# Two more quarters of the array for the values of an attention step, and a new order of the step, on one core

## The reference

```python
qkv = x @ Wqkv; q, k, v = split(qkv)            # 128 -> 3 * 1024
q, k = l2norm(q) * qs, l2norm(k) * ksc          # per head, then rotary with a scale
sim = einsum('bhwie,bhwje->bhwij', bq, bk2) * 8 # a window of 32 looks at itself and the one before
attn = softmax(where(mask, -max, sim))
x = x + einsum('bhwij,bhwje->bhwie', attn, bv2).reshape(b, n, 1024) @ Wo
xn = (x - mu) / sqrt(var + 1e-5) * g + bln
a, gate = split(xn @ W1 + b1)                   # 128 -> 2 * 341
x = x + (a * gelu(gate)) @ W2 + b2
```

## Time and profile before

| | before |
|---|---|
| median of three runs | 2670.35 us (2667.77 to 2670.66) |
| the profiled execution | 2670.37 us, span 2668.6 us |
| TensorE busy | 2405.0 us, 90% |
| ScalarE busy | 1779.9 us, 67% |
| VectorE busy | 1754.0 us, 66% |
| GpSimd busy | 1407.7 us, 53% |
| mean granted clock of TensorE | 0.951 of full speed |

### The profile page before, as it was taken

How to read it: one execution, slowest core, us unless ns; L and a number is a source line. 1 busy time by engine, 2 the same in 40 slices (tenths; PEclk the granted TensorE clock), 3 DMA queues, 4 the chain that set the end, 5 groups by cost and what they waited for, 6 DMA issues and landing times.

```text
span 2668.6 us, 94059 instructions
## 1 busy us (share of the span) xinstructions
PE 2405.0 (90%) x36344; PEld 1671.1 (63%) x36344; DVE 1754.0 (66%) x4841; ACT 1779.9 (67%) x6116; POOL 1407.7 (53%) x1358
## 2 busy tenths in 40 slices
PE   6997899999999999999999999999998676799996
PEld 4664676666666666666666666666666354566662
DVE  3554776777767766777767777777774324788863
ACT  3774677777767776777767777777776142678771
POOL 1664665666556565656565655666563000666650
PEclk9999999999999999999999999999999676899997
DMA  3000112111121113111121113111121100000000
GB/s 96 1 0 3 32 42 76 39 39 39 40 69 41 38 37 77 39 38 38 36 75 38 40 36 79 39 40 38 39 59 36 29 0 4 9 15 16 13 10 20
DMA packets 143994, 97.15 MB, mean 36 GB/s; under 512 B 67112, under 2 KB 138320, under 8 KB 142800
## 3 DMA queue, kind: packets, MB, share of 16 engines
q1 hardware_dynamic: 143568, 91.31, 13.4%
HBM read 23.11 MB, written 1.05 MB: 9 GB/s over the span
## 4 chain that ended last, share of the span: by engine, by line
PE 76%; ACT 9%; issue 7%; DVE 3%; SPq 2%; POOL 1%; DMA 1%; ACTq 0%; POOLq 0%; DVEq 0%
PE bank L668 20%; PE bank L745 10%; PE bank L778 7%; PE bank L689 7%; PE bank L723 5%; PE bank L832 3%; PE bank L823 3%; PE bank L732 3%; PE bank L814 2%; PE bank L390 2%; PE bank L653 2%; PE bank L717 2%; ACT L1252 1%; ACT arena L1252 1%; PE bank L764 1%
## 5 line engine op out<-in xcount | busy, mean ns | idle before, releaser
L1430 POOL TENSOR_TENSOR arena<-arena 128x512 f32<-128x512 f32 x448 | 561.2, 1272 | 416.3 <-DVE arena L1570 416.3
L668 PE MATMUL bank<-wqkv,hs 128*128 128x512 f32 x1344 | 671.1, 609 | 41.1 <-ACT arena L1233 29.0
L1437 POOL TENSOR_TENSOR arena<-arena,rnorm 128x512 f32<-128x512 f32 x448 | 458.8, 1044 | 93.4 <-DVE rnorm L1619 91.3
L1565 DVE TENSOR_TENSOR arena<-bank,rot 128x512 f32<-128x512 f32 x448 | 308.5, 689 | 233.0 <-PE bank L668 216.6
L1204 ACT ACTIVATE arena<-bank,amx 128x64 f32<-128x64 f32 x1536 | 458.4, 336 | 0.3
L1444 POOL TENSOR_TENSOR arena<-arena,ainv 128x512 f32<-128x512 f32 x192 | 200.4, 1044 | 365.5 <-DVE ainv L1642 365.5
L668 PEld LDWEIGHTS bank<-wqkv,hs 128*128 128x128 f32 x1344 | 231.8, 195 | 210.1 <-issue 153.0
L745 PE MATMUL bank<-arena 64*64 64x32 f32 (+1 forms) x9216 | 315.0, 221 | 47.1 <-issue 30.1
L745 PEld LDWEIGHTS bank<-arena 64*64 64x64 f32 x9216 | 291.1, 136 | 101.8 <-issue 60.2
L1204 ACT ACTIVATION_READ_ACCUMULATOR arena<-bank,amx 128x1 f32 x1536 | 353.1, 230 | 0.0
L1233 ACT ACTIVATE arena<-bank 128x512 f32<-128x512 f32 x224 | 133.4, 596 | 321.1 <-PE bank L745 284.4
(11 more groups left out here) (160 smaller groups left out, 3514.8 us busy)
## 6 DMA issues: line engine op xcount, KB each, us to landing
arena<-arena SPq DMA_DIRECT2D x384, 64.0 KB, 2.4
arena<-arena SPq DMA_DIRECT2D x768, 32.0 KB, 1.9
wqkv<-in_L_ffn_Wqkv_dram SPq DMA_DIRECT2D x6, 1024.0 KB, 5.2
hs<-z SPq DMA_DIRECT2D x128, 32.0 KB, 1.8
fx<-z SPq DMA_DIRECT2D x32, 128.0 KB, 2.3
hs<-z SPq DMA_DIRECT2D x128, 31.8 KB, 1.9
fx<-z SPq DMA_DIRECT2D x32, 127.0 KB, 2.5
wqkv<-in_L_ffn_Wqkv_dram SPq DMA_DIRECT2D x24, 128.0 KB, 5.4
```

The lines of the kernel that those rows point to most:

```text
L668: nc.tensor.matmul(bank[o][:], src[:], wqkv[w][:, off:off + 512], start=True, stop=True).then_inc(AT[name] if part < 2 else AT[name][i], 1)
L1430: nc.gpsimd.tensor_tensor(t, t, rs[i][c], ALU.add).then_inc(AT["ak" if c else "aq"][i], 1)
L1437: nc.gpsimd.tensor_tensor(t, t, rnorm[p % 2][:, i, HU * c:HU * c + HU].unsqueeze(2).to_broadcast([P, HU, DH]), ALU.mult).then_inc(AT["mk" ...
L1565: nc.vector.tensor_tensor(heads(rc[i][c][p % 2]), src, r[:, 2 * c, :].unsqueeze(1).to_broadcast([P, HU, DH]), ALU.mult)
```

## The change

Four parts, all in phase 0 alone:
- values_all computes the four chunks in two halves. Chunks 0 and 1 go, as all did, from rows of group g to the columns and partitions of the same numbers in bank 7. Chunks 2 and 3 go to the other partitions (group 0 to 64 to 127, group 1 to 0 to 63) of bank 6. The calls alternate between the four quarters of the array. The number of matmuls is the same.
- In o_t chunks 2 and 3 thus have their partitions swapped. The rows of the output weights are loaded to match, by six DMAs for a layer where there was one. The waits on ld_wo count six.
- outputs copies 256 columns of bank 7 and 256 of bank 6.
- The lists step_0 of TensorE, ScalarE, GpSimd and VectorE have a new order. values_all(0) takes batch s-2 where it took s-3, and so do values_all(1), probs_all(1), project_out, outputs and the residual; scores(0), values(0), exponents(0) and divide(0) take s-1 where they took s-2; turn(1) of queries takes s-1 where it took s-2. Waits follow: the new bank 6 work waits for the copy of the keys and is waited for by the next keys and probabilities. SyncE's list is not changed.

The diff; of the lists the new text alone is shown (the lines taken out are those of the lists printed above):

```diff
@@ -496,8 +496,11 @@
                     sp.dma_start(qks[:, j, :], A[pre + n][i].rearrange("(o d) -> o d", o=1).to_broadcast([P, DH])
                                  ).then_inc(ld_rot, 16)
                 if ph["net"] == 0:
-                    sp.dma_start(wo[w][:].rearrange("p a b n -> p (a b) n"), A[pre + ph["Wo"]][i].rearrange("(j p) n -> p j n", p=P)
-                                 ).then_inc(ld_wo, 16)
+                    wo_ = A[pre + ph["Wo"]][i].rearrange("(u v j p) n -> v p u j n", u=2, v=2, p=P)
+                    for u in range(2):
+                        sp.dma_start(wo[w][:, u, 0:2, :], wo_[0][:, u]).then_inc(ld_wo, 16)
+                        for a in range(2):
+                            sp.dma_start(wo[w][DH * a:DH * a + DH, u, 2:4, :], wo_[1][DH * (1 - a):DH * (1 - a) + DH, u]).then_inc(ld_wo, 16)
                 else:
                     wo_ = A[pre + ph["Wo"]][i].rearrange("(j a g d) n -> a g d j n", a=2, g=2, d=DH)
                     for a in range(2):
...
@@ -738,12 +741,13 @@
                     pe.wait_ge(vd[i], 96 * (p + 1))
                     v, b, c = v_s[i], vb[i][:, 0:256], vb[i][:, 256:512]
                     sources = [((0, 64), (v[:, 0:256], b)), ((64, 96), (c, c)), ((96, 128), (b, v[:, 256:512]))]
-                    for j in range(4):
+                    for j in range(2):
                         for (q0, q1), src in sources:
-                            for g in range(2):
-                                rows = slice(DH * g, DH * g + DH)
-                                mm = nc.tensor.matmul(bank4[7][rows, j, q0:q1], src[g][rows, DH * j:DH * j + DH],
-                                                      pbt[i][0][rows, j * P + q0:j * P + q1], start=True, stop=True)
+                            for half in range(2):
+                                for g in range(2):
+                                    rows, to, h = slice(DH * g, DH * g + DH), DH * (g ^ half), j + 2 * half
+                                    mm = nc.tensor.matmul(bank4[7 - half][to:to + DH, j, q0:q1], src[g][rows, DH * h:DH * h + DH],
+                                                          pbt[i][0][rows, h * P + q0:h * P + q1], start=True, stop=True)
                     mm.then_inc(AT["o"][i], 1)
 
                 def probs(i, p, g):
...
@@ -870,78 +874,83 @@
                         ff_up(f, slot_ - 2, s)
 
                 def step_0(s):
                     if live(s):
                         if live(s - 1):
                             at(pe, AT["sqk"], un(1, s - 1))
                         keys(0, s)
                     if live(s - 2):
                         if live(s - 3):
                             at(pe, AT["res"][0], s - 2)
                         else:
                             at(pe, AT["ve"][0], s - 1)
                         project_in(1, s - 2, 2, 7, "v")
+                        at(pe, AT["qte"][1], s - 1)
+                        probs_all(0, s - 2)
+                    if live(s):
+                        if live(s - 1):
+                            at(pe, AT["sqq"], un(1, s - 1))
+                        queries(0, s)
+                    if live(s - 2):
+                        at(pe, AG["ex"][0][0], s - 1)
+                        at(pe, AG["ex"][0][1], s - 1)
+                        scores_all(1, s - 2)
+                        at(pe, AT["ve"][1], s - 1)
+                        at(pe, AT["kte"][1], s - 1)
+                        values_all(0, s - 2)
+                    feed_forward_0(s, 0)
+                    if live(s):
+                        at(pe, AT["sqk"], un(0, s))
+                        keys(1, s)
+                    if live(s - 1):
                         if live(s - 2):
                             at(pe, AG["pte"][0][0], s - 1)
                         turn(0, s - 1, 0, "mq", "qt")
+                    feed_forward_0(s, 1)
+                    if live(s - 1):
+                        if live(s - 2):
+                            at(pe, AT["oe"][0], s - 1)
+                        elif live(s - 3):
+                            at(pe, AT["oe"][1], s - 2)
+                        turn(0, s - 1, 1, "mk", "kt")
+                        if live(s - 2):
+                            at(pe, AT["oe"][0], s - 1)
+                        elif live(s - 3):
+                            at(pe, AT["res"][0], s - 2)
+                        project_in(0, s - 1, 2, 7, "v")
+                    if live(s):
+                        at(pe, AT["sqq"], un(0, s))
+                        queries(1, s)
+                    if live(s - 2):
+                        if live(s - 1):
+                            at(pe, AT["kte"][0], s)
+                        else:
+                            at(pe, AT["oe"][0], s - 1)
+                        probs_all(1, s - 2)
+                    if live(s - 1):
+                        if live(s - 2):
+                            at(pe, AG["ex"][1][0], s - 1)
+                            at(pe, AG["ex"][1][1], s - 1)
+                        scores_all(0, s - 1)
+                    if live(s - 2):
+                        if live(s - 1):
+                            at(pe, AT["ve"][0], s)
+                        else:
+                            at(pe, AT["oe"][0], s - 1)
+                        at(pe, AG["pte"][1][0], s - 1)
+                        values_all(1, s - 2)
                     feed_forward_0(s, 2)
+                    if live(s - 1):
+                        at(pe, AT["qte"][0], s)
+                        turn(1, s - 1, 0, "mq", "qt")
+                    if live(s - 2):
+                        at(pe, AT["oe"][1], s - 1)
+                        project_out(s - 2, (0, 1), 0)
+                    if live(s - 1):
+                        if live(s - 2):
+                            at(pe, AT["oe"][1], s - 1)
+                        else:
+                            at(pe, AT["kte"][0], s)
+                        turn(1, s - 1, 1, "mk", "kt")
 
                 def step_1(s):
                     if live(s):
@@ -1230,7 +1239,12 @@
                         at(act, AT["y"][0], p)
                     else:
                         at(act, AT["y"][i], nth(i, p - 1))
-                    nc.scalar.activation(o_t[i], bank[7][:], ACT.Copy).then_inc(AT["oe"][i], 1)
+                    if ni == 0:
+                        for half in range(2):
+                            ins = nc.scalar.activation(o_t[i][:, 256 * half:256 * half + 256], bank[7 - half][:, 0:256], ACT.Copy)
+                        ins.then_inc(AT["oe"][i], 1)
+                    else:
+                        nc.scalar.activation(o_t[i], bank[7][:], ACT.Copy).then_inc(AT["oe"][i], 1)
 
                 def ff_square(f):
                     act.wait_ge(FF["cen"], f + 1)
...
@@ -1254,37 +1268,36 @@
 
                 def step_0(s):
                     c, f, before = ff_phase(ph, s)
+                    if live(s - 2):
+                        turned(1, s - 2, 1)
+                        probs_all(0, s - 2)
+                        values(1, s - 2)
                     if live(s):
                         square(0, s, 1)
+                    if live(s - 2):
+                        outputs(0, s - 2)
+                        exponents_all(1, s - 2)
                     if live(s):
                         square(0, s, 0)
+                    if live(s - 1):
+                        turned(0, s - 1, 1)
+                        turned(0, s - 1, 0)
+                        values(0, s - 1)
+                    if live(s):
+                        square(1, s, 1)
+                    if live(s - 2):
+                        probs_all(1, s - 2)
                     if c == 0 and f >= 0:
                         ff_square(f)
                     if c == 1 and f >= 0:
                         ff_affine(f)
                     if live(s):
                         square(1, s, 0)
                     if live(s - 2):
+                        outputs(1, s - 2)
+                    if live(s - 1):
+                        exponents_all(0, s - 1)
+                        turned(1, s - 1, 0)
                     if c == 2 and f >= 0:
                         ff_gelu(f)
 
@@ -1453,21 +1466,22 @@
 
                 def step_0(s):
                     if live(s - 1):
+                        add(1, s - 1, 1)
+                    if live(s):
+                        add(0, s, 1)
+                    if live(s - 1):
+                        normal(0, s - 1, 0)
                         normal(1, s - 1, 1)
                         normal(0, s - 1, 1)
                     if live(s - 2):
+                        divide_all(1, s - 2)
                     if live(s - 1):
                         normal(1, s - 1, 0)
+                    if live(s):
+                        add(0, s, 0)
                         add(1, s, 0)
+                    if live(s - 1):
+                        divide_all(0, s - 1)
 
                 def step_1(s):
                     if live(s - 2):
```

(32 more changed lines are left out.)

96 lines of the change are left out of this document (4 added, 92 removed).

## The result

| | before | changed |
|---|---|---|
| median | 2670.35 us (2667.77 to 2676.25, 5 runs) | 2683.6 us (2680.42 to 2693.41, 5 runs) |
| ratio, 95% interval | | 1.0059 (1.0033 to 1.0086) |
| span of the profiled execution | 2668.6 us | 2681.5 us |

The forecast was 2608 us.

What follows compares the result with a forecast made beforehand. Phase 0 was taken as bound by TensorE's matmul stream, busy 1379 of 1450 us. The sum was 2670.4 - 134.4 (quick values) + 44 (waits) + 36 (reloads) - 8 (ends) = 2608 us, range 2545 to 2662.

Steps and rivals of the forecast that it cites:

- Part 1: values_all in four quarters of TensorE's array: 0.82 us a call for 1.52, saving 134 us over 192 calls.
- the 60-cycle figure: Skill's overhead per matmul: 48 passes of values_all would need 1.2 us, leaving less than a third of the gain.
- Part 2: New order of a step: 4.35 us of waits in four steps against 2.5 before, +44 us in the sum.
- the walk: Hand trace of the five engines' new lists through four steps, giving where waits fall and 4.35 us of them.
- the prediction's one round: Four profiled steps from 1200.21 to 1273.71 us: 73.5 us, with 2.5 us of waits for other engines.
- the slower rival: Array quarters take turns, values_all stays at 1.52 us, longer stream fills about 1.45 us of waits: 2708 us, 8%.
- Part 3: Six weight reloads on SyncE's queue delay the value copies: about 10 us each where 4 now, +36 us.
- Part 4: Ends: one thin step fewer, -8 us; instruction fetches inside values_all: 0, at worst +14 us.
- the clock: Rival: waits in step c=3 cost each round 4 us at half clock, +48 us: 2656 us, 15%.
- the waits and the reloads: Two cost terms of the sum: +44 us for the new order's waits, +36 us for the six weight reloads.

Runs made afterwards that it cites:

- e1: New order of a step alone, with values_all, output copy and output-weight load as in the kernel before: 2763.1 us, ratio 1.0349.
- e5: Changed kernel with one idle 0.86 us matmul between each scores_all and the values_all behind it: 2774.1 us, ratio 1.0388.
- e12: Kernel before, with its weight DMAs spread over five steps: 2670.9 us, ratio 0.9996.
- e4: Changed kernel with scores_all and values_all apart: values_all(0) behind keys(1), query transposes of unit 1 before values_all(1): 2769.8 us, ratio 1.0359.
- e7: Changed kernel with merged score pieces, four value-copy DMAs for six, and weight DMAs spread over five steps: 2568.7 us, ratio 0.9631.
- e6: Kernel before, with two 32-column score matmuls merged into one of 64 and four value-copy DMAs for six: 2595.5 us, ratio 0.9716.
- e10: e7 with the query transposes of unit 1 between scores(0) and values_all(1): 2596.9 us, 28 more than e7.

## Why the prediction was wrong

- Part 1, 0.82 us for values_all, was right to 0.01 us. That tiles run beside each other and that one needs 58 ns a pass could be read from the scores' rows; the estimate (1.2 us) from the 60-cycle figure of the Trainium skill, TensorEngine Tiling (Array Packing), section Performance Considerations, was not borne out.
- Part 2: the waits came where the walk put them. Before scores(1) of c=3 it was 1.11 us in this round, on ScalarE's copy behind GELU (1.65 forecast); before queries(1) 0.54 us, on the square (0.6 forecast):

```profile
1485.03 0.30 PE L720 MATMUL bank<-mask_b,ident_b 64*32 64x256 bf16 x8 [1.11 <-ACT arena L1190]
...
1492.10 1.12 PE L671 MATMUL bank<-wqkv,hs 128*128 128x512 f32 x2 [0.54 <-ACT arena L1184]
```

  From 450 to 1900 us the waits for other engines come to 2.9 us in four steps in the mean, 4.35 forecast, and to 2.3 in the kernel before, 2.5 by the prediction's one round: the size was too large by 29 us. Clean steps of 15.6 to 17 us are in the trace. The walk and the slower rival took it that a longer stream fills some of these waits. It does not: in 96 steps they are 70 us with the slow values (e1), 70 with the quick ones, 75 with the filler (e5). A stop is not made good in them either: the stops are added to the steps in full.
- Part 3: the mechanism was right. SyncE's weight DMAs and the copies behind them, then TensorE:

```profile
1638.47 0.34 SPq L487 DMA_DIRECT2D wqkv<-in_L_ffn_Wqkv_dram  x1
...
1655.22 3.71 SPq L578 DMA_DIRECT2D arena<-arena  x6
```

```profile
1660.36 1.50 PE L749 MATMUL bank<-arena 64*64 64x64 f32 x48 [9.30 <-DMA arena<-arena]
1661.79 2.07 PE L794 MATMUL bank<-fx,mean_w 128*128 128x512 f32 x2
1663.65 1.74 PE L671 MATMUL bank<-wqkv,hs 128*128 128x512 f32 x2
```

  16.7 us of weight DMAs (15.5 forecast), 9.3 us of waiting, and behind it two projections' time for one (the granted clock from 1661.8 to 1665.3 is 0.53). This is the longest of four such waits in the stretch; the others are 3.0, 5.5 and 7.1, the mean 6.2 us (7.6 forecast). In the kernel before there are 5.0 us in the same four reloads, not 2.7 in each. The term was also added up wrong: it counts the same 2 us of slow clock before and after, so its own numbers give 6 x (7.6 - 2.7) = 29 us, not 36. Spreading the DMAs gave 19 us, in the kernel before nothing where it had "4" for each (e12), since stops came in place of part of the waits.
- The step that failed is in Part 4, on instruction fetches: "the consumer is faster now, the bytes are the same; 0, at worst +14". It priced a stop by the time by which values_all got shorter, and held their number fixed. Both grew, from 24 to 60 and from 32 to 83 us, and their term came out at +68 us: 256 records of scores and values are now used up in 1.77 us (1475.74 to 1477.51 above), where a stop ends about 2.5 us after the packet with the next ones has started, and the new order has such a run twice in a step. (The expectation of e4 speaks of 544 records; there are 272.) That this could happen stood in the rows: 0.94 us of "issue" inside a loop that waits for nothing, right behind the scores, as 18 of the 24 are. I had seen the row and counted it as a constant.
- The second failure is the clock. It was a rival of its own, tied to the waits of step c=3. It came instead at stops and reloads: of the 15 stretches at half clock from 450 to 1900 us, 12 begin in a stop or within 2.1 us behind one, and three at a reload's wait. In all it was 102 us at half clock, against 44. e5 and e7, with fewer stops, have 34 and 24. It cost +15 us by the account, beside the 12 us that the new order's own stream is longer, which no term had.
- The slower rival, with turns among the quarters, did not happen. The time came out on its side by another road: the quick part was quick, and its speed outran the supply.
- Errors of opposite sign are in the sum: the waits and the reloads were priced 40 us too high, which hid part of what the stops, the clock and the small slips cost.

Open: how far ahead of the end of a block the next is asked for, why spreading the weight DMAs brought more stops, and where the small slips and the 12 us of the new order's stream come from. That e1 has twice the stops of before because it has twice the places is a count that fits; no run has the new order with one of the two places taken away and nothing else moved.

## What to carry to other kernels

When a dense run of small instructions is made faster, or comes more often, count its records: in this kernel a stop inside a loop that waits for nothing, at the same place in every 256 records, was the supply of instructions, and it grew with speed (e1 to the changed kernel: 55 to 83 us). Fewer and larger instructions were worth more here than better packed ones (e6: 16 of 80 records off a group, 2.8% of the whole), and they made the packed version pay as well (e7: 3.7%). Whoever shortens a pipeline by a step should look at what stands on the DMA queue ahead of the transfer that is now needed a step earlier.

## What the runs showed of the hardware

- A 64x64 tile of the array takes about 58 ns for a float32 pass with its weight load (a mix of 32 and 64 columns), with one other tile at work or with three: 48 passes in 1.52 us on two quarters, in 0.83 us on four. The 58 ns is an estimate from these, with 0.12 us taken off for the change of shape.
- TensorE's instructions come in blocks of 256 records (16 KB); a stop ends some 2.5 us after the last block's packet starts. 0.86 us of slow work ahead of the values brings the stops there from 52 in 153 groups to 23 in 145 (e5); 0.44 us of transposes leaves them, 21 in 80 against 22 in 81 (e10).
- Stops cost twice: beside their own length the granted clock falls to 0.5 (1.2 GHz) at some of them. 58 us more of half clock came with 51 us more of stops and 20 us more of DMA waits; with the stops down from 83 to 25 us (e5) it went from 102 to 34 us, though the DMA waits stayed (25.9 us).
- Two copies of 256 columns out of PSUM take ScalarE 381 ns each, one of 512 takes 596 ns: 0.17 us more for the two, where the prediction had 0.25.
